# A fused layer-norm, attention and mixture-of-experts kernel: projection weights loaded at the program's start, and the layer-norm's small steps moved and merged

## The reference

```python
x = L0_attn_x                                   # [16, 2048, 1024] f16
xn = _layernorm(x, axis=-1)
s = _L0_attn_ref(xn, qw, kw, vw, ow)            # 16 heads, rope on Q and K, causal, f32 softmax
g = _silu(_L0_ffn_ref(xn, Wg, We, be))          # 8 experts, the 2 best of each token, weighted
return x + s * g

def _layernorm(x, axis=-1, eps=1e-5):
    m = jnp.mean(x, axis=axis, keepdims=True)
    v = jnp.var(x, axis=axis, keepdims=True)
    return (x - m) / jnp.sqrt(v + eps)
```

## Time and profile before

| | us |
|---|---|
| median of three runs | 3153.36 |
| lowest of the three | 3152.33 |
| the profiled execution | 3144.91 |
| its span on the slowest core, core 3 | 3143.4 |
| spans of the eight cores | 3129.5 to 3143.4 |

### The profile page before, as it was taken

How to read it: one execution, slowest core, us unless ns; L and a number is a source line. 1 busy time by engine, 2 the same in 40 slices (tenths; PEclk the granted TensorE clock), 3 DMA queues, 4 the chain that set the end, 5 groups by cost and what they waited for, 6 DMA issues and landing times.

```text
span 3143.4 us, 29388 instructions; the slowest of 8 cores (3129.5 to 3143.4 us)
## 1 busy us (share of the span) xinstructions
PE 2153.1 (68%) x9720; PEld 797.3 (25%) x9720; DVE 1053.7 (34%) x1496; ACT 940.2 (30%) x1245; POOL 538.7 (17%) x575
## 2 busy tenths in 40 slices
PE   0000349888669959978995994477778826777787
PEld 0000313333224424433442442011121101121212
DVE  5700136666624414432441442132121113221212
ACT  4500012222210020010002001345758704657574
POOL 1100017888800000000000000211111102111111
PEclk9999999999879979988997997577888865888888
DMA  3499432322264254315606334420201070220100
GB/s 91 119 114 134 80 99 96 112 102 101 101 117 64 44 109 79 54 42 93 108 1 134 54 54 131 85 67 0 67 11 43 1 172 17 67 67 1 54 1 27
DMA packets 418115, 229.08 MB, mean 73 GB/s; under 512 B 376480, under 2 KB 376480, under 8 KB 417456
## 3 DMA queue, kind: packets, MB, share of 16 engines
q1 hardware_dynamic: 403184, 159.54, 23.9%
q0 software_dynamic: 14784, 67.66, 9.4%
HBM read 92.67 MB, written 75.76 MB: 54 GB/s over the span
## 4 chain that ended last, share of the span: by engine, by line
PE 44%; DVE 13%; ACT 11%; SPq 8%; issue 8%; DMA 7%; POOL 5%; another core or an unknown queue 3%; POOLq 0%; DVEq 0%; ACTq 0%
PE PA L639 14%; PE PB L639 14%; ACT AR L823 8%; SPq L238 7%; PE PV L742 5%; POOL AR L834 4%; PE PA L868 4%; DMA AR<-c_sin 3%; PE PA L813 2%; PE PB L813 2%; DVE AR L535 2%; DVE AR L541 2%; DMA xn_sp<-AR 2%; ACT AR L752 2%
## 5 line engine op out<-in xcount | busy, mean ns | idle before, releaser
L639 PE MATMUL PA<-AR 128*128 128x512 f16 x2048 | 472.6, 385 | 21.6 <-DMA AR<-we 21.6
L742 PE MATMUL PV<-AR 128*128 128x512 f16 (+6 forms) x1280 | 418.2, 418 | 66.5 <-POOL AR L834 66.4
L639 PE MATMUL PB<-AR 128*128 128x512 f16 x2048 | 462.9, 379 | 0.0
L823 ACT ACTIVATE AR<-PA 128x1024 f16<-128x1024 f32 x320 | 303.0, 947 | 246.5 <-PE PA L813 244.5
L813 PE MATMUL PA<-AR 64*128 64x512 f16 x640 | 149.1, 457 | 290.8 <-ACT AR L823 142.1
L649 DVE SCALAR_TENSOR_TENSOR AR<-PA,wm,AR 128x512 f32<-128x512 f32 x256 | 192.2, 751 | 423.3 <-PE PA L639 226.5
L834 POOL TENSOR_TENSOR AR<-AR,tri 128x256 f16<-128x256 f16 x256 | 170.7, 667 | 815.2 <-ACT AR L823 791.3
L823 ACT ACTIVATE AR<-PB 128x1024 f16<-128x1024 f32 (+1 forms) x320 | 276.1, 863 | 91.2 <-PE PB L813 90.9
L649 DVE SCALAR_TENSOR_TENSOR AR<-PB,wm,AR 128x512 f32<-128x512 f32 x256 | 192.2, 751 | 249.6 <-PE PB L639 231.8
L639 PEld LDWEIGHTS PA<-AR 128*128 128x128 f16 x2048 | 202.7, 99 | 271.4 <-issue 36.2
L784 DVE TENSOR_TENSOR AR<-AR,PC 64x512 f16<-64x512 f32 x64 | 43.5, 679 | 662.0 <-PE PC L778 661.5
(11 more groups left out here) (97 smaller groups left out, 1838.5 us busy)
## 6 DMA issues: line engine op xcount, KB each, us to landing
we<-we POOLq DMA_DIRECT2D x8, 2048.0 KB, 89.0
out_c<-AR SPq DMA_DIRECT2D x8, 2048.0 KB, 9.0
v_sp<-AR POOLq DMA_DIRECT2D x32, 264.0 KB, 3.1
AR<-v_sp POOLq DMA_DIRECT2D x2, 4224.0 KB, 25.9
AR<-x_c POOLq DMA_DIRECT2D x32, 256.0 KB, 2.8
xn_sp<-AR SPq DMA_DIRECT2D x32, 256.0 KB, 2.0
AR<-c_cos SPq DMA_DIRECT2D x32, 256.0 KB, 2.7
AR<-c_sin SPq DMA_DIRECT2D x32, 256.0 KB, 3.0
```

The source lines that it names most:

```text
L639: sl=slots[ib], half=half: e.matmul(PG[:, 512 * ib:512 * ib + 512], lhs, sl[:, c * D + half * 512: c * D + (half + 1) * 512], start=(c == ...
L742: nkc=nkc, p2=p2, mw=mw: e.matmul(PV2[0:mw, 512 * p2 + w0:512 * p2 + 512], v_sb[:, kc * VF + h * VW:kc * VF + h * VW + mw], expb3[sbk][:, ...
L823: W("scalar", lambda e, PS=PS, sbk=sbk, ev=ev: e.activation(ev(expb3[sbk]), ev(PS), AF.Exp, scale=1.0 / 32.0), waits=[("eT", C["eT"]), ("e ...
```

## The change

Three edits in `build_nc`.

- **Weights.** The loads of `qwS`, `kwS` and `vwS` are now the first three transfers of SP, ahead of the constants, and wait for nothing. To make room, the layer-norm's buffers (`xst`, `xc32`, `sqd`, `xn16`) and the gate's `lgall` and `l2a` lie 71,680 bytes further up in `AR2`. The three loads behind the barrier and the waits `p1w` go.
- **Mean.** The scaling and the negation of the row sum are done by GpSimd, under its own semaphore `eP`, and ScalarE waits for that. The row sum (now L292) waits for VectorE's previous operation.
- **Small steps.** Epsilon is added with an f16 output, without the cast behind it; the square root writes f16 itself, without the cast behind it.

The diff, with the addresses and the waits for the spills (now in the list `spall`) left out:

```diff
+        dma("sync", qwS[:, :].rearrange("k (c n) -> k c n", c=NCH),
+            qw_h.rearrange("(c k) n -> k c n", k=128), "sw3")
+        dma("sync", kwS[:, :].rearrange("k (c n) -> k c n", c=NCH),
+            kw_h.rearrange("(c k) n -> k c n", k=128), "sw3")
+        dma("sync", vwS[:, :].rearrange("k (c n) -> k c n", c=NCH),
+            vw_h.rearrange("(c k) n -> k c n", k=128), "sw3")
         dma("sync", tri[:, :], tri_h[:, :], "scst")
...
-              waits=[(SX[q], C[SX[q]]), ("eV", tok.get(("mrd", q), 0))],
+              waits=[(SX[q], C[SX[q]]), ("eV", C["eV"])],
               inc="eV")
-            W("vector", lambda e, q=q: e.tensor_scalar(
+            W("gpsimd", lambda e, q=q: e.tensor_scalar(
                 m16[q][:, :], m32[q][:, :], 1.0 / D, None, op0=ALU.mult),
-              waits=[("eV", C["eV"])], inc="eV")
-            W("vector", lambda e, q=q: e.tensor_scalar(
+              waits=[("eV", C["eV"]), ("eP", C["eP"])], inc="eP")
+            W("gpsimd", lambda e, q=q: e.tensor_scalar(
                 mneg[q][:, :], m16[q][:, :], -1.0, None, op0=ALU.mult),
-              waits=[("eV", C["eV"])], inc="eV")
-            tok[("mnegd", q)] = C["eV"]
+              waits=[("eP", C["eP"])], inc="eP")
+            tok[("mnegd", q)] = C["eP"]
...
-              waits=[("eV", tok[("mnegd", q)]),
+              waits=[("eP", tok[("mnegd", q)]),
...
-                s32t[q][:, :], v16t[q][:, :], EPS16, None, op0=ALU.add),
-              waits=[("eV", C["eV"])], inc="eV")
-            W("vector", lambda e, q=q: e.tensor_copy(s16t[q][:, :],
-                                                     s32t[q][:, :]),
+                s16t[q][:, :], v16t[q][:, :], EPS16, None, op0=ALU.add),
...
-            W("scalar", lambda e, q=q: e.activation(r32t[q][:, :],
+            W("scalar", lambda e, q=q: e.activation(r16t[q][:, :],
                                                     s16t[q][:, :], AF.Sqrt),
...
-            W("vector", lambda e, q=q: e.tensor_copy(r16t[q][:, :],
-                                                     r32t[q][:, :]),
-              waits=[("eA", tok[("sqrtd", q)]), ("eV", C["eV"])], inc="eV")
             W("vector", lambda e, q=q: e.reciprocal(rc32[q][:, :],
                                                     r16t[q][:, :]),
-              waits=[("eV", C["eV"])], inc="eV")
+              waits=[("eA", tok[("sqrtd", q)]), ("eV", C["eV"])], inc="eV")
...
-        p1w = P.bw() + [("sspA", C["sspA"]), ("sspB", C["sspB"]),
-                        ("sspC", C["sspC"]), ("sspD", C["sspD"])]
-        dma("sync", qwS[:, :].rearrange("k (c n) -> k c n", c=NCH),
-            qw_h.rearrange("(c k) n -> k c n", k=128), "sw3", waits=p1w)
-        dma("sync", kwS[:, :].rearrange("k (c n) -> k c n", c=NCH),
-            kw_h.rearrange("(c k) n -> k c n", k=128), "sw3")
-        dma("sync", vwS[:, :].rearrange("k (c n) -> k c n", c=NCH),
-            vw_h.rearrange("(c k) n -> k c n", k=128), "sw3")
```

More of the change, by code:

```diff
@@ L148, in build_nc @@
         attnT = c16(AR1, 49152, 8192)
[L150 to L155, removed]
+        xst = [c16(AR2, 71680 + 2048 * i, 1024) for i in range(4)]
+        xc32 = [c32(AR2, 79872 + 4096 * i, 1024) for i in range(4)]
+        sqd = c32(AR2, 96256, 1024)
+        xn16 = [c16(AR2, 100352 + 2048 * i, 1024) for i in range(4)]
+        lgall = c32(AR2, 108544, 256)
+        l2a = c32(AR2, 109568, 256)
         qwS = c16(AR2, 0, 8192)
@@ L367, in build_nc @@
         dma("gpsimd", be16s[0:8, :], be_h[:, :], "sbe")
+        spall = [("sspA", C["sspA"]), ("sspB", C["sspB"]),
+                 ("sspC", C["sspC"]), ("sspD", C["sspD"])]
         for c in range(NCH):
@@ L371, in build_nc @@
                 xn_sp[:, c * 128:(c + 1) * 128], "sxnT", transpose=True,
-                waits=[("sspA", C["sspA"]), ("sspB", C["sspB"]),
-                       ("sspC", C["sspC"]), ("sspD", C["sspD"])])
+                waits=spall)
         xnT_rd = C["sxnT"]
```

## The result

The changed kernel takes 3188.33 us (median of nine runs) against 3153.17 for the kernel before (ten runs): a ratio of 1.012, with a 95% interval of 1.010 to 1.014. It is slower by about 1.2%; forecast were 3187 and 1.1%. Some executions of every kernel here run with one die or both at a lower granted clock (0.77 instead of 0.88 in the longest of the changed kernel) and take several per cent more; the ratios leave them out. The profiled execution's slowest core is core 2, with a span of 3184.8 against 3143.4, and the eight spans lie between 3173.3 and 3184.8.

A forecast was written before the change was run, and what follows sets the result against it. The prediction took the layer-norm's turn, which delays GpSimd's cast issue, and the cast's full DMA engines as the bound; 60.9 - 3 - 23.6 = +34 us gave 3187 us, 1.1% more, range 3162 to 3218.

The forecast's parts named there:

- what decides its end is when GpSimd issues the cast: Stage before the transposing loads: its end follows GpSimd's issue of the expert-weight cast, which stands behind the last x load.
- The weights, what goes: At the first projection matmul: without weight loads behind the gate's barrier it starts 23.6 us sooner, at 420.25 instead of 443.89.
- The weights, what comes: At the kernel's start: constants wait behind the weight loads, so the split of gate weights starts 19.5 us later, near 26.
- The ring: Layer-norm: each x load waits for the mean, the mean for the row sum, that for the previous load; 5.4 us a turn.
- The bounds of 4.6 and 6.5: Lowest and highest layer-norm turn in us, from short or long GpSimd operations and steps; +12 and +65 us in total.
- From the cast to the transposing loads: From the cast's issue to the first transposing load: between 150 and 160 us, 157 taken, 3 less than before.
- The sum: Whole kernel: 60.9 us later cast, minus 3 behind it, minus 23.6 at the projections, gives +34 us.
- That GpSimd's issue is held up for 1.0 us: Rival, layer-norm: load issue waits for VectorE's cast and scaling, turn 6.4, 28 us more, 3216 us; chance 0.15.
- That the constants aren't held up: Rival, kernel start: constants land as early as before beside the weights, 19.5 us goes, +15, 3168 us; chance 0.10.
- That VectorE sets the turn: Rival, layer-norm: x loads keep ahead of row sums, turn 3.6 us, -16 us, 3137 us, not slower; chance 0.06.

## Why the prediction was right

**Where the stage's end is decided.** The step "what decides its end is when GpSimd issues the cast" carried the sum, and is now shown and not only argued: in ten kernels with the uncut cast in its old place, issued between 131.5 and 252.9 us, the first transposing load followed 157 to 163 later, and where the cast was moved away, it came at 143.

**The weights, what goes**: 23.6, measured 24 in the run that has this alone. Right.

**The weights, what comes**: 19.5. The split started 19.4 later in the profiled execution of the change, 21.1 to 22.9 later in four experiments with the weights first (27.71, 28.44, 28.82, 29.53). The value was right for one, 2 to 3 us low for the others. That the start would be paid in full, since ScalarE's copies stand behind it, was right.

**The ring.** 5.33 reckoned, 5.4 taken, 5.57 measured. Its terms, from the turn above: the sum 1.22 (1.21), to GpSimd 0.23 (0.22), the two operations 0.42 (0.30), between them 0.15 (0.15), to the issue 0.30 (0.55), from issue to row sum 3.14 (2.9). That adds up to 5.46, the turn of 132.79; the others differ by the last term, 3.20 in the median and up to 3.65, where the issue itself took 1.03. Two terms were off by a quarter of a us and cancelled, which was luck: an issue behind an operation on whose end it doesn't wait starts after 0.30, and a load is used later than I took it to be. Of that last 0.2 to 0.3 us 0.1 is the issue held by the cast; why loads land after 3.0 us in the median instead of 2.8, also with their issue clear of the cast, isn't shown. The operations themselves, 0.42 for 0.30, are half of what was missing in the sum. The bounds of 4.6 and 6.5 were far wider than what the operations of 128x1, the least known of them, deserved: 0.21 each.

**From the cast to the transposing loads**: 157 against 156.9.

**The sum.** +34 against +37.4 at the first projection matmul. The 28 turns of 0.17 account for 4.8 more, the rest gave 1.4 back. That the time was met within 2 us is in part luck: the medians grew by 35.2, but the two profiled executions, from which the steps are read, by 41.4, and the 4.0 behind the projections were in no term.

**The rivals.** That GpSimd's issue is held up for 1.0 us fell by the run with the load behind the scaling; the issue is held up, but by 0.09 in most turns. That the constants aren't held up fell by the split at 26.00. That VectorE sets the turn is what happens when the loads stand two ahead: the run gave 0.9944, where 3137 had been reckoned for it, a ratio of 0.995. The mechanism that the change was written for exists, and its reckoned price was right; it was not what this order of the queue let happen.

## What to carry to other kernels

A queue that issues loads in advance must hold nothing that waits for one of those loads: two operations of 0.21 us put between them cost 2.0 us in each of 28 turns here (5.57 against 3.57 with the loads two ahead), since every load then waited for the one before. When a transfer is moved to the start of a queue, ask what stands behind it and who waits for that; the same weights behind three small loads cost the layer-norm nothing with four loads of x in flight, and 4 us with one. And in a stage where the DMA engines are full, look for what sets its start: moving the bulk transfer behind the work that shares its engines gave 61 us, more than every saving on the compute engines, and 27 more once the projections no longer waited for its end.

## What the runs showed of the hardware that I had not expected

GpSimd's drain at a barrier came only when the transfers that it had issued were done: 151.38 us behind the last issue, the length of the cast, and the wait was gone when the mark stood ahead of the issues. In the kernel before it was hidden, as the cast was over before the gate.

The rows of a bulk transfer set what others pay beside it: a store of 256 KB took 33 to 42 us beside a cast in rows of 16384 elements, and 10 to 13 beside the same cast in rows of 512.

An issue on GpSimd that runs beside a cast of VectorE took 0.58 us or until 0.12 behind the cast's end, whichever was later.

The cast of the expert weights also slowed the gate's 768 matmuls, from 26 us to 50 (190.1 to 240.4 on the slowest core), with 28 us of TensorE's idle time put down to issue, in five gaps. The trace has one transfer of 16,384 bytes on a queue of instructions in each gap, landing 1.1 to 1.3 us before TensorE goes on; without the cast beside them the same transfers come and no gap does. That points to the fetch of instructions; no run was made on it.
